# First stage from centred input, token-sliced splits, rates picked by matmul, and joined orders in the scan

## The reference, cut to what matters

```
XQ, XK, XV = x @ q_w.T, x @ k_w.T, x @ v_w.T          # per head: chunks of 16 tokens
ttt_lr_eta = sigmoid(x @ ttt_lr_weight + bias) / 16    # the rates
step(W, b), for each of the 32 chunks:
    Z = xk @ W + b;  grad = ln_fused_l2_bwd(Z, xv - xk, ln_w, ln_b)
    out = xq + ln(xq @ W - eta * tril(xq @ xk.T) @ grad + (b - tril(eta) @ grad))
    W -= (last_eta * xk).T @ grad;  b -= sum(last_eta * grad)
```

## Time and profile before

| what | value |
|---|---|
| median of 3 runs | 2010.04 us (2007.79 to 2011.96) |
| profiled execution | 2006.43 us |
| its span in the trace | 2004.8 us |
| TensorE busy | 1875.6 us, 94% |
| VectorE, ScalarE, GpSimd busy | 1224.2, 979.8, 1022.7 us |
| DMA | 297.96 MB, mean 149 GB/s |
| first stage | start to about 191 us, next block from about 195 us |
| scan stage | first `z_product` at 198.9 us, 32nd at 727.5 us, outputs to about 834 us |

### The profile page before, as it was taken

The page is one execution under the profiler, slowest core; times in us unless marked ns, Lnnn a source line. Parts: engine busy times, 40 slices in busy tenths (PEclk is TensorE's granted clock), DMA queues, the critical chain, the costliest instruction groups (busy, mean ns, idle before and its releaser), DMA issues. The chain is left out here.

```text
span 2004.8 us, 34531 instructions
## 1 busy us (share of the span) xinstructions
PE 1875.6 (94%) x12504; PEld 1414.9 (71%) x12504; DVE 1224.2 (61%) x2415; ACT 979.8 (49%) x2115; POOL 1022.7 (51%) x894
## 2 busy tenths in 40 slices
PE   5898999998999999799999989999999999999998
PEld 3676777666666665488778866777777777777776
DVE  4563566788788874467344456666666666666663
ACT  3332556566665655445444335444444444444442
POOL 5444566556565654420243347555555555555552
PEclk9899999999999999989999999999999999999999
DMA  7785657436334533232789841222323233322320
GB/s 243 275 297 191 230 169 262 123 110 220 119 114 150 190 117 97 73 108 92 239 258 289 290 176 54 88 113 95 123 99 116 95 105 117 116 83 73 107 98 30
DMA packets 157111, 297.96 MB, mean 149 GB/s; under 512 B 20240, under 2 KB 97296, under 8 KB 150288
## 3 DMA queue, kind: packets, MB, share of 16 engines
q1 hardware_dynamic: 155856, 294.70, 43.7%
q10 hardware_dynamic: 1088, 1.05, 0.2%
HBM read 221.52 MB, written 74.19 MB: 148 GB/s over the span
## 5 line engine op out<-in xcount | busy, mean ns | idle before, releaser
L2005 POOL TENSOR_SCALAR probs<-probs,rsum 128x512 f32<-128x512 f32 x256 | 396.1, 1565 | 249.0 <-DVE rsum L2141 249.0
L2105 ACT ACTIVATE p_tok<-bank 128x512 fp32r<-128x512 f32 x256 | 154.5, 606 | 346.4 <-PE bank L2045 346.3
L2137 DVE TENSOR_REDUCE nmax<-bank 128x1 f32<-128x512 f32 x256 | 158.9, 683 | 95.2 <-PE bank L2037 95.2
L2147 DVE TENSOR_TENSOR p_tok<-bank,p_tok 128x512 fp32r<-128x512 f32 x256 | 173.3, 680 | 16.1 <-ACT p_tok L2105 16.1
L2097 ACT ACTIVATE probs<-bank,nmax 128x512 f32<-128x512 f32 x256 | 172.8, 692 | 3.2 <-DVE nmax L2137 3.2
L60 PE MATMUL bank<-xs,ffn_w 128*128 128x512 f32 x352 | 152.9, 434 | 6.7 <-issue 3.4
L2045 PE MATMUL bank<-ident,probs 128*128 128x128 f32 x1024 | 156.5, 277 | 2.8 <-DVE p_tok L2147 2.8
L1493 POOL TENSOR_TENSOR y_pieces<-y_tok,y_pieces 128x512 fp32r<-128x512 f32 x48 | 66.1, 1393 | 181.9 <-ACT y_pieces L1698 181.9
L2045 PEld LDWEIGHTS bank<-ident,probs 128*128 128x128 f32 x1024 | 122.3, 141 | 51.1 <-issue 27.5
L61 PE MATMUL bank<-xs,ffn_w 128*128 128x512 f32 x352 | 138.8, 394 | 0.0
L62 PE MATMUL bank<-xs,ffn_w 128*128 128x512 f32 x352 | 138.6, 394 | 0.0
(11 more groups left out here) (281 smaller groups left out, 4951.4 us busy)
## 6 DMA issues: line engine op xcount, KB each, us to landing
ffn_w<-ffn_pieces SPq DMA_DIRECT2D x120, 512.0 KB, 3.8
uvo<-uvo_pieces SPq DMA_DIRECT2D x15, 2048.0 KB, 8.6
wq<-wq_pieces SPq DMA_DIRECT2D x16, 1536.0 KB, 6.5
ffn_pieces<-stage SPq DMA_DIRECT2D x30, 512.0 KB, 4.1
xs<-xn_pieces SPq DMA_DIRECT2D x4, 2048.0 KB, 8.1
y_tok<-in_gup SPq DMA_DIRECT2D x32, 256.0 KB, 3.6
wk<-wk_pieces SPq DMA_DIRECT2D x16, 512.0 KB, 3.6
ffn_w<-ffn_pieces SPq DMA_DIRECT2D x16, 384.0 KB, 3.5
```

What stands on the lines that cost most here:

```text
L2005: nc.gpsimd.tensor_scalar(probs[:, u % 8, :], probs[:, u % 8, :], rsum[:, u % 8:u % 8 + 1], None, ALU.mult).then_inc(norm_done, 1)
L2105: nc.scalar.activation(p_tok[:, Q % 2, 0, :, hh * P:(hh + 1) * P], banks[4 + u % 2][:].rearrange("p (k q) -> p k q", k=NBLK), ACT.Copy).th ...
L2137: nc.vector.tensor_reduce(nmax[:, u % 8:u % 8 + 1], banks[u % HG][:], axis=X_AXIS, op=ALU.max, negate=True).then_inc(max_done, 1)
L2147: nc.vector.tensor_tensor(p_tok[:, Q % 2, 1, :, q], banks[4 + u % 2][:].rearrange("p (k q) -> p k q", k=NBLK), p_tok[:, Q % 2, 0, :, q].bi ...
```

## The change

In words, by part:

1. **Tile 0.** K and Q are projected from `xc` before it is divided by the deviation. ScalarE and VectorE split the centred input into `first_hi` and `first_lo` (in parts of `k_t` that tile 0 does not write), and eight evictions, all on VectorE now, multiply by the inverse deviation (`scaled`). V is projected from the normalised input as before. TensorE's order is K0, K1, variance, K2, K3, Q0, mean of tile 1, Q1, first part of the rates, Q2, second part, Q3, V0, variance of tile 1, V1 to V3. The order of the other engines and of SyncE's loads is written out anew for tile 0.
2. **Splits by token slices.** `split_x(t)` and `split_low(t, j)` take 128 tokens of all four groups at a time, each as soon as the V job of the tile before that reads this slice is done, instead of waiting for all jobs.
3. **Rates in two parts.** `rate_parts(t)` ahead of K, `rate_sums(t)` behind the first K job.
4. `scan_constants` stands in the last tile, behind `rates`.
5. **Rates picked.** 64 small matmuls with a 0/1 matrix (`pick_rates`, ahead of the last Q jobs) and one copy out of PSUM replace the move through HBM.
6. **Early loads.** `xs` and `ffn_w` get fixed homes over the K and V weights; their first loads stand in the first stage (SyncE after the last K jobs, ScalarE's queue after the last V jobs), and the scan block starts with the first four trips.
7. **Scan orders.** From step 9 to 31 the trips are dealt (9, 2, 2, 0) instead of (8, 2, 2, 1); `scores` of the second part stands ahead of `base`; `spread_q` of a step's first part stands at the end of the step before.

```diff
+        NWP, NEARLY = 5, 4
+        xs_in, fw_in = sem("ttt_xs_in"), [sem(f"ttt_fw_in{i}") for i in range(NWP)]
...
+            xs = nc.alloc_sbuf_tensor_at("xs", [P, 2, NF, TB], F32R, offset=first_home)
+            fw = nc.alloc_sbuf_tensor_at("ffn_w", [P, NWP, 2, NF, P], F32R, offset=first_home + 16 * 1024)
...
-            on_act = lambda J: jobs[J][0] == "K"
+            on_act = lambda J: jobs[J][0] == "K" and jobs[J][1] > 0
...
+                    for r in range(NRAW, NRAW + NF):
+                        load_raw(r)
+                    load_x(1)
+                    for r in range(NRAW + NF, 2 * NRAW):
+                        load_raw(r)
                     for dst, src in loads:
                         sp.dma_start(dst, src).then_inc(pc_in, 16)
-                    load_x(1)
-                    for i in range(NW):
-                        for r in raw_of[i]:
-                            load_raw(r + NRAW)
+                    for r in range(2 * NRAW, 3 * NRAW):
+                        load_raw(r)
...
-                    def move_rates():
-                        sp.wait_ge(sig_done, 2)
-                        for b in range(BATCH):
-                            sp.dma_start(lr_dram[b].rearrange("(m n) t e x -> (n t) m (e x)", m=NF), lr_raw[:, NF * b:NF * b + NF, :]).then_inc(lr_out, 16)
-                        sp.wait_ge(lr_out, 16 * BATCH)
-                        for b in range(BATCH):
-                            for e in range(2):
-                                c = 32 * b + 16 * e
-                                sp.dma_start(lr[c:c + 16, :, :], lr_dram[b].rearrange("n t e x -> t e n x")[:, e, :, :]).then_inc(lr_in, 16)
+                    def load_first_xs():
+                        sp.wait_ge(job_ready, JT * (NTB - 1) + NF)
+                        sp.wait_ge(xs_out, 32)
+                        sp.dma_start(xs[:].bitcast(F32), xs_pc[0]).then_inc(xs_in, 16)
...
-                    for i in range(NW):
-                        if pieces[i][0] == "kvw":
...
+                    for i in range(2 * NF):
+                        low(i)
+                    target(2 * NF)
+                    for i in range(2 * NF, NW):
+                        if i + 1 < NW:
+                            target(i + 1)
                         low(i)
...
+                    def pick_rates():
+                        pe.wait_ge(pick_in, 16)
+                        pe.wait_ge(sig_done, 2)
+                        pe.wait_ge(std_done, NTB)
+                        for c in range(P // CHUNK):
+                            for e in range(2):
+                                for b in range(BATCH):
+                                    ins = nc.tensor.matmul(banks[5][32 * b:32 * b + 32, c * NF * NX:(c + 1) * NF * NX], pick[:, c, e, :],
+                                                           lr_raw[:, NF * b:NF * b + NF, e * NX:(e + 1) * NX],
+                                                           start=(e == 0), stop=(e == 1), skip_group_check=True)
+                        ins.then_inc(picked, 1)
...
+                    project(0, "K", 0)
+                    project(0, "K", 1)
                     var(0)
+                    project(0, "K", 2)
+                    project(0, "K", 3)
+                    project(0, "Q", 0)
+                    mean(1)
+                    project(0, "Q", 1)
                     pe.wait_ge(lrw_in, 32)
...
+                    for t in range(1, NTB):
+                        rate_parts(t)
+                        for j in range(NF):
+                            project(t, kinds(t)[0], j)
+                            if j == 0:
+                                rate_sums(t)
...
                     def split_x(t):
+                        act.wait_ge(y_done, NF * (t + 1))
                         if t >= 1:
-                            act.wait_ge(job_ready, JT * t)
                             act.wait_ge(xs_out, 32 * t)
-                        for k in range(NF):
-                            act.wait_ge(y_done, NF * t + k + 1)
-                            nc.scalar.activation(xs_hi[:, k, :], xc[:, k, :], ACT.Copy).then_inc(hi_done, 1)
+                        for j in range(NF):
+                            c = slice(j * P, (j + 1) * P)
+                            if t >= 1:
+                                act.wait_ge(job_ready, job_at(t - 1, "V", j) + 1)
+                            nc.scalar.activation(xs_hi[:, :, c], xc[:, :, c], ACT.Copy).then_inc(hi_done, 1)
 
                     for i in range(NF):
                         high(i)
+                    first_split()
                     squares(0)
-                    for i in range(NF, NW - NF):
+                    for i in range(NF, 2 * NF):
                         high(i)
                     act.wait_ge(ready, 3)
                     deviation(0)
+                    for i in range(2 * NF, NW - 1):
+                        high(i)
+                    split_x(0)
+                    high(NW - 1)
+                    rates(0)
+                    squares(1)
+                    splits(0, 0)
+                    deviation(1)
+                    splits(0, 1)
+                    splits(0, 2)
...
+                    act.wait_ge(job_ready, JT * (NTB - 1) + 2 * NF)
+                    for w in range(NEARLY):
+                        act.wait_ge(st_out[w % NST], 16 * (w // NST + 1))
+                        n = width(JOBS_T[w])
+                        act.dma_start(fw[:, w, :, 0:n, :].bitcast(F32), fw_pc[w][:, :, 0:n, :]).then_inc(fw_in[w], 16)
...
+                    def scaled(kind, j):
+                        J = job_at(0, kind, j)
+                        dve.wait_ge(job_ready, J + 1)
+                        nc.vector.tensor_tensor((k_t if kind == "K" else q_t)[:, j, 0:TB], banks[J % 4][:], std[:], ALU.mult).then_inc(ev_dve, 1)
...
+                    first_low()
+                    sum_squares(0)
+                    sum_x(1)
+                    invert(0)
+                    for j in range(NF):
+                        scaled("K", j)
                     normalize(0)
+                    for j in range(NF):
+                        split_low(0, j)
+                    scaled("Q", 0)
+                    scaled("Q", 1)
+                    center(1)
+                    scaled("Q", 2)
+                    scaled("Q", 3)
+                    sum_squares(1)
+                    rates(0)
+                    keep_v(0, 0)
+                    invert(1)
+                    normalize(1)
...
-            share = lambda n: (11, 3, 2, 2) if n < LAG else (8, 2, 2, 1) if n < NSTEP else (2, 2, 1, 1)
+            share = lambda n: (11, 3, 2, 2) if n < LAG else (9, 2, 2, 0) if n < NSTEP else (2, 2, 1, 1)
...
+                    for x in range(NF):
+                        trip(x)
                     turn_k(0)
...
                         ffn(n, 2)
+                        if ps:
+                            scores(ps[1])
                         G = opens_at(n)
                         if G is not None:
                             base(G)
-                        if ps:
-                            scores(ps[1])
                         ffn(n, 3)
...
                             late(n - 1)
-                        if ps:
-                            spread_q(ps[0])
                         ffn(n, 0)
...
                         ffn(n, 2)
+                        if parts_at(n + 1):
+                            spread_q(parts_at(n + 1)[0])
```

More of the change, by code:

```diff
@@ L518, in _, with first_low, split_low @@
                     nc.vector.memset(eps[:, 1:2], TTT_EPS).then_inc(ready, 1)
+                    def first_low():
+                        for k in range(NF):
+                            dve.wait_ge(fhi_done, k + 1)
+                            nc.vector.tensor_tensor(first_lo[k][:], xc[:, k, :], first_hi[k][:].bitcast(F32), ALU.subtract).then_inc(flo_done, 1)
+                    def split_low(t, j):
+                        c = slice(j * P, (j + 1) * P)
+                        dve.wait_ge(hi_done, NF * t + j + 1)
+                        nc.vector.tensor_tensor(xs_lo[:, :, c], xc[:, :, c], xs_hi[:, :, c].bitcast(F32), ALU.subtract).then_inc(lo_done, 1)
@@ new lines, in _ @@
+                    for j in range(NF):
+                        split_low(0, j)
[9 more added lines that the diff above has]
+                    normalize(1)
+                    for j in range(1, NF):
+                        keep_v(0, j)
+                        split_low(1, j - 1)
@@ new lines, in _ @@
+                    split_low(1, NF - 1)
+                    for t in range(1, NTB - 1):
+                        sum_x(t + 1)
+                        rates(t)
+                        center(t + 1)
+                        sum_squares(t + 1)
+                        for j in range(NF):
+                            keep_q(t, j)
+                        invert(t + 1)
+                        normalize(t + 1)
+                        for j in range(NF):
```

(14 more changed lines are left out.)

222 lines of the change are left out of this document (110 added, 112 removed).

## The result

The changed kernel takes 1995.3 us (median of 4 runs, 1992.5 to 2000.7) against 2009.3 for the kernel before in the same session: a ratio of 0.9927 (0.9901 to 0.9953), 14 us faster. A second set of the same kernel gave 0.9934 (0.9913 to 0.9954). The forecast was 29 us, a time of 1981 with a range from 1971 to 1992: the direction is right, the size is half, and the time lies outside. The cause lies for the most part in the first stage, where VectorE had to wait for GpSimd.

A forecast was written before the change was run, and what follows sets the result against it. TensorE was taken as busy nearly everywhere, so only its idle time could be won: first stage 8.5, seam 9.8, steps 9 to 31 6, last steps 5, together 29.3 us, giving 1981 us, range 1971 to 1992.

The forecast's parts named there:

- K(1) at 67.7: First stage: K of tile 1 starts at 67.7 us, 10.2 earlier than 77.88.
- one low slice and its order 0.6: Tile 1: after the last high slices, VectorE's last low slice and its order take 0.6 us before K starts.
- V to K 2.0 in tiles 2 and 3: First stage: K starts 2.0 us after the last V matmul instead of 3.75, gaining 1.6 over both tiles.
- a tile 2 that starts at full clock: First stage: bound of 4 us on the gain of tiles 2 and 3 if tile 2 no longer starts slow.
- the weight pieces rule tile 0: Rival, chance 0.17: full DMA engines hold tile 0's pieces, K of tile 1 at about 73, total 1986 us.
- Picking 2.4: Tile 3: picking the rates by 64 small matmuls adds 2.4 us on the path, bounds 1.2 and 5.
- The seam 9.8: From the first stage's end to scan step 1's first product (z(1)): 9.8 us shorter, bounds 5 and 11.
- 8.5: End of TensorE's last first-stage job (E): 8.5 us earlier, at 182.5 instead of 191.0.
- Steps 9 to 31, 6: Scan: one trip moved ahead of the state update wins 6 us, range 0 to 12.
- Last steps 5: Last scan steps: moving `spread_q` earlier removes waits on `q_bd` and wins 5 us, range 0 to 6.3.
- ScalarE as the bound: Rival, chance 0.04: ScalarE bounds the scan step, 22 steps lose 2.0 us each, total 2031, slower.
- One sum of a bound: Tile 0's bound of 15.8 us: inverse and normalisation end at 58.2, seven evictions and 0.6 slices give 62.1.

The follow-up runs named there:

- joined: Changed kernel with GpSimd's products behind VectorE's low slices, ScalarE's split of tile 1 before three weight pieces, 2 MB load behind last stores; 1985.6 us, 0.9882.
- joined_order: joined with SyncE issuing four of the last tile's eight constants stores and the 2 MB input load behind them; 1990.7 us, 0.9900.
- scan_only: The kernel before with only the three edits of order in the scan; 2002.7 us, 0.9965.
- scan_again: The program of scan_only run once more for a second profile; 2000.9 us, 0.9946.

## Why the prediction was wrong

- **K(1) at 67.7, and "one low slice and its order 0.6": the step that failed.** Measured 72.96. From the last high slice to K(1) it was 5.0 and not 0.6, for a slice had to wait for GpSimd's products and took 1.15 to 1.75, and two V evictions stand between the slices, which I had not counted. I had the price of "instructions of that size" from centring, 2.48 for four with GpSimd busy beside it, but centring reads one input from a bank. The low halves of tile 0, both inputs in SBUF and GpSimd beside them, were there to be read in the trace of before, at nearly twice that:

```profile
25.46 4.65 DVE L529 TENSOR_TENSOR xs_lo<-xc,xs_hi 128x512 fp32r<-128x512 f32 x4
```

- **V to K 2.0 in tiles 2 and 3: the same fault.** Measured 4.6, and the longer idle time let the clock fall on K's first jobs. Together these made E 12.8 later than forecast (5.3 up to K(1), 7.5 from there); without the contention it is 182.1 (forecast 182.5). That this is so close is in part luck: K(1) is 69.3 there, still 1.6 late, and from K(1) to E it is 2.0 shorter than forecast, with picking at 1.93 and a tile 2 that starts at full clock, which the forecast had only as a bound.
- **The rival "the weight pieces rule tile 0"** named the right K(1) (73) and half of the cause: the pieces hold the split until the products begin, the contention does the rest.
- **Picking 2.4:** 1.93 measured. **The seam 9.8:** 8.6, with the first trip late on its weights by 2.25. The second profile of the same program has 21.8, so 6.8. Behind an E of 180 to 182 it gave less (22.7 to 25.4), because stores, input and first weights had not all landed before 184 to 187 in any of the joined kernels. The forecast's 8.5 and 9.8 do not add: even joined reaches z(1) at 203.5, forecast 201.3.
- **Steps 9 to 31, 6:** the share of trips does give about 6 (4.4 to 8); I had set the moved spread and base at nothing in this stretch, and together they cost about 3, by one profile; and the clock, of which I had said nothing here, takes 1 to 5 in one execution and another.
- **Last steps 5:** 5.3, by the spread, as forecast. **ScalarE as the bound:** its wait for the z product falls from 56.7 to 21.3 but does not vanish; it is not the bound, and the scan is not slower.
- In the two profiles the sum is off by 20.0: 12.8 at E, 1.2 at the seam, 5.8 in steps 9 to 31, 2.1 in code that is the same, less 1.9 in the other stretches; by the medians by 15.
- One sum of a bound is off by 0.3: seven evictions and slices of 0.6 behind 58.2 end at 62.4, not at 62.1. Nothing hangs on it.

## What to carry to other kernels

Before you take an engine's duration from a row, look at what GpSimd did beside it, and price a moved VectorE operation that reads SBUF twice with the GpSimd instruction that it will meet: it ends when that one has ended and its own work is done. If the two meet, make the one that nobody waits for wait. Gains ahead of a meeting of the engines are worth only as much as the last transfers allow: look at when they move, not only at when they are issued. And when a change of a few us in a scan is weighed, read the granted clock first, with more than one profile of the same program.

## What the runs showed of the hardware

- VectorE's subtraction with both inputs in SBUF (128x512, float32) took 0.68 or 0.69, 0.60 from start to start, when no GpSimd instruction was running as it began. When one was (132 times), it ended 0.54 to 0.57 behind that one's end, so that its own length was 0.68 to 1.78. GpSimd's products, 1.26 to 1.32 alone, ended 1.12 to 1.16 behind the slice that was running as they began. VectorE's addition with one input from PSUM, between those slices, kept its 0.68. The Trainium skill, GPSIMD Engine Reference, "Key points", has the two engines share their SBUF interfaces, with contention when a VectorE instruction has two SBUF inputs: the trace agrees, and shows the price, a wait for the other's end.
- The same program (scan_only and scan_again), with its longer idle times on TensorE alike within 0.1 us, was granted 1.00 of the clock in steps 9 to 31 in one execution and 0.98 in another, 6.3 us apart, of which 4.3 lie in slow feed-forward matmuls.
- In joined_order 1 MB of stores in packets of 1 KB stood ahead of 4 MB of loads in both queues; nine tenths of it had moved 3.9 us after the last was issued, but the wait for all of it ended 9.5 us after. In joined the stores of one queue moved nothing for 4.7 us while a 2 MB load of the other queue, issued 0.6 us earlier, was moved.
